# Causal attention with a gated feed-forward part on one core: transposes two steps behind the scores instead of three

## The reference, cut to what matters

```python
q = einsum('bse,hde->bhsd', x, Wq) + bq        # k and v in the same way
scores = einsum('bhsd,bhtd->bhst', q, k) / scale
scores = where(causal, -inf, scores)
att = softmax(scores, axis=-1) / scale
z = einsum('bhst,bhtd->bhsd', att, v)
return z.reshape(b, s, h * dh) @ proj
```

## Time and profile before

| what | value |
|---|---|
| median of three runs | 1347.55 us |
| the profiled execution's own time | 1347.42 us |
| its span, first to last instruction | 1345.7 us |
| PE busy | 1330.3 us, 99% of the span |
| DVE, ACT, POOL busy | 82%, 81%, 74% of the span |
| granted TensorE clock over the span | 1.000 of full speed |

### The profile page before, as it was taken

How to read it: one execution, slowest core, us unless ns; L and a number is a source line. 1 busy time by engine, 2 the same in 40 slices (tenths; PEclk the granted TensorE clock), 3 DMA queues, 4 the chain that set the end, 5 groups by cost and what they waited for, 6 DMA issues and landing times.

```text
span 1345.7 us, 34453 instructions
## 1 busy us (share of the span) xinstructions
PE 1330.3 (99%) x10783; PEld 1131.7 (84%) x10783; DVE 1106.3 (82%) x4001; ACT 1085.9 (81%) x3162; POOL 997.7 (74%) x1443
## 2 busy tenths in 40 slices
PE   7999999999999999999999999999999999999998
PEld 5788888888888888888888888888888888888887
DVE  8978888788787878878788787888878888788785
ACT  6887887888788887887888788788888887888785
POOL 7887777778777777777777768777677876778664
PEclk9999999999999999999999999999999999999999
DMA  6455444544544445454444544454454454545541
GB/s 155 95 119 118 103 112 113 122 104 111 125 107 116 105 113 123 103 122 110 116 103 115 123 103 115 112 122 110 103 124 113 103 122 112 122 95 119 118 103 48
DMA packets 112561, 150.59 MB, mean 112 GB/s; under 512 B 18239, under 2 KB 47230, under 8 KB 112382
## 3 DMA queue, kind: packets, MB, share of 16 engines
q1 hardware_dynamic: 111086, 147.97, 46.8%
q10 hardware_dynamic: 1296, 0.42, 0.2%
HBM read 10.69 MB, written 4.19 MB: 11 GB/s over the span
## 4 chain that ended last, share of the span: by engine, by line
PE 95%; ACT 1%; SPq 0%; POOL 0%; DVE 0%; DMA 0%; issue 0%; DVEq 0%; POOLq 0%
PE zp L1323 22%; PE ptp L1297 20%; PE jobp L1167 13%; PE scores L1285 9%; PE scores L1288 7%; PE outp L1335 7%; PE jobp L1172 6%; PE scores L1266 4%; PE scores L1263 3%; PE jobp L1182 1%; PE outp L1344 1%; PE jobp L1187 1%; PE jobp L1360 0%; PE jobp L1177 0%; ACT prob L721 0%; PE outp L1349 0%
## 5 line engine op out<-in xcount | busy, mean ns | idle before, releaser
L632 POOL TENSOR_TENSOR prob<-prob,rden 128x128 f32<-128x128 f32 (+3 forms) x1024 | 712.4, 720 | 247.2 <-DVE rden L971 240.7
L982 DVE CUSTOM_DVE_ANT_0 prob<-scores,mask 128x128 f32<-128x128 f32 (+3 forms) x1024 | 471.7, 488 | 199.8 <-issue 133.3
L721 ACT ACTIVATE prob<-prob,nmax 128x128 f32<-128x128 f32 (+3 forms) x1024 | 567.5, 559 | 12.1 <-DVE nmax L982 5.4
L1297 PE MATMUL ptp<-ident,prob 128*128 128x128 f32 x2560 | 366.9, 274 | 2.1 <-ACT pt L732 1.5
L1297 PEld LDWEIGHTS ptp<-ident,prob 128*128 128x128 f32 x2560 | 295.0, 140 | 27.4 <-POOL prob L632 5.0
L1323 PE MATMUL zp<-pt,v_sb 128*64 128x64 f32 (+3 forms) x4096 | 307.7, 303 | 0.0
L732 ACT ACTIVATE pt<-ptp 128x128 f32<-128x128 f32 (+3 forms) x512 | 221.2, 432 | 102.8 <-PE ptp L1297 102.8
L1323 PEld LDWEIGHTS zp<-pt,v_sb 128*64 128x64 f32 x4096 | 221.6, 137 | 51.2 <-issue 19.7
L994 DVE COPY pt<-ptp 128x128 f32<-128x128 f32 (+3 forms) x512 | 243.3, 475 | 3.9 <-PE ptp L1297 3.1
L571 POOL CAST k_low<-k_lo 64x512 fp32r<-64x512 f32 x256 | 156.0, 609 | 78.0 <-DVE k_lo L866 68.1
L1285 PE MATMUL scores<-k_twice,q_parts 128*128 128x384 f32 (+1 forms) x512 | 200.9, 392 | 0.0
(11 more groups left out here) (192 smaller groups left out, 2003.3 us busy)
## 6 DMA issues: line engine op xcount, KB each, us to landing
k_twice<-k_hi SPq DMA_DIRECT2D x506, 128.0 KB, 2.3
q_parts<-q_lo SPq DMA_DIRECT2D x256, 128.0 KB, 2.4
q_parts<-q_hi SPq DMA_DIRECT2D x254, 128.0 KB, 2.3
xin<-in_L_attn_x_dram SPq DMA_DIRECT2D x16, 256.0 KB, 3.1
xres<-in_L_attn_x_dram SPq DMA_DIRECT2D x16, 256.0 KB, 3.1
out_dram<-osb SPq DMA_DIRECT2D x15, 256.0 KB, 2.6
pt<-in_L_attn_Wq_dram SPq DMA_DIRECT2D x1, 512.0 KB, 4.8
pt<-in_L_attn_Wk_dram SPq DMA_DIRECT2D x1, 512.0 KB, 5.6
```

The lines of the kernel that those rows point to most:

```text
L632: nc.gpsimd.tensor_tensor(part, part, scale, ALU.mult).then_inc(pn_ready, 1)
L721: nc.scalar.activation(part, part, ACT.Exp, bias=nmax[:, s % NROT, h:h + 1], scale=-1.0, accum_out=den[:, s % NROT, h:h + 1]).then_inc(p_r ...
L982: nc.vector.tensor_tensor_reduce(out=prob[:, s % NROT, h, 0:cols], in0=scores[bank][:, first_col:first_col + cols], in1=mask[:, S - cols:S ...
L1297: done = nc.tensor.transpose(ptp[h][:, P * j:P * j + P], prob[:, s % NROT, h, P * j:P * j + P], ident[:])
```

## The change

LAG_T goes from 3 to 2. The transposes of unit s now stand in PE's step s+2, behind the scores of unit s+2, and the two copies of the transposed unit move with them on ACT and DVE. The value products keep their nine steps, and so do all other lags. The tail loses the transposes and copies of unit -3, since the last batch's own steps now reach that unit. The number of instructions on each engine stays the same.

```diff
-LAG_T = 3
+LAG_T = 2
...
-            evacuate_pt(c, -3)
             evacuate_z(c, -2)
             evacuate_pt(c, -2)
...
             reciprocals(c, -1)
-            evacuate_pt(c, -3)
             evacuate_pt(c, -2)
...
-            transpose(c, -3)
             project(c, -2, 2)
```

## The result

The changed kernel takes 1541.14 us (median of six runs, 1540.27 to 1543.08) against 1347.77 us for the kernel before (six runs, 1347.40 to 1348.26): a ratio of 1.1437, 95% interval 1.1423 to 1.1452. It is 193.4 us slower; forecast were 174.5 us more, 1522 in a range of 1465 to 1572. The profiled execution took 1542.95 us, with a span of 1541.2.

A forecast was written before the change was run, and what follows sets the result against it. PE, busy 1330.3 of 1345.7 us, was taken as the bound, so its waits are paid in full. Span 1345.7 + 159 (pairs) + 16 (once a batch) = 1520.7, plus 1.7 around it: 1522 us, range 1465 to 1572.

The forecast's parts named there:

- Which unit waits, where and for whom: PE's transposes of 512- and 256-column units wait for POOL's rows, 256 to 512 places, 150 to 200 us in total.
- Unit 15, 0.25 + 0.56: 512-column unit: PE's transposes wait 0.25 us for POOL's head 0 and 0.56 for head 1, together 0.81.
- Unit 17, 0.07 + 0.36: 256-column unit: PE's transposes wait 0.07 us for POOL's head 0 and 0.36 for head 1, together 0.43.
- Each pair pays again: DVE and POOL slip together with PE, so every pair of heads costs 1.24 us; 128 pairs cost 159 us.
- A single slip: Rival: after a first wait of about 1 us the engines stay ahead of PE; 1343 to 1348 us, chance 0.03.
- The ring: Rival: late transposes delay copies, exponentials, second maximum and next reciprocal; 50 to 90 us on top, 1575 to 1610, chance 0.12.
- Once a batch, +1.0 us: POOL's router products delay unit 3, +0.5 us; other steps an estimated +0.5; 16 us over 16 batches.
- Other widths nothing: Units of 128 and 384 columns: value products or 0.22 us more cover stand ahead of their transposes; counted as nothing.
- Second-order terms nothing: Wider DVE copies and ACT's copy ahead of the exponentials eat some 0.2 of 0.4 us slack; counted as nothing.
- The clock stays: PE keeps 2.4 GHz despite waits; the rival, a fall to 1.2 GHz throughout, meant above 2600 us, chance 0.02.
- The bounds: Lower: second heads alone, 0.95 a pair, 122 us, 1469; upper: 1.55 a pair, 1.6 more a batch, 224 us, 1572.
- the four rivals: Copies delaying reciprocals, 0.12; only second heads late, 1430 to 1450 us, 0.08; one slip only, 0.03; PE's clock falling, 0.02.

The follow-up runs named there:

- experiment 1: Changed kernel, with POOL multiplying only the first half of each head's columns: 1379.51 us.
- experiment 7: Changed kernel, with one more POOL multiplication of 128 columns, into an unread tile, ahead of each 512-column unit: 1582.63 us.
- experiment 2: Changed kernel, with DVE's reciprocals of 512- and 256-column units ahead of both maxima of the next unit: 1461.42 us.
- experiment 3: Changed kernel, with DVE's copy of the transposed head behind both maxima in steps with i = 3: 1540.94 us.
- experiment 4: Changed kernel, with PE's transposes of the 512-column unit between the value products of head 0 and head 1: 1556.03 us.
- experiment 10: Changed kernel, 512-column transposes behind both heads' value products, those units' copies last on DVE and ACT, 256-column reciprocal ahead of the next maxima: 1498.81 us.
- the best reordering: Changed kernel, 512-column transposes between the heads' value products, those units' copies last on DVE and ACT, 256-column reciprocal ahead of the next maxima: 1430.65 us.
- experiment 9: Kernel before (lag three), with value products cut in two around transposes and job, and that step's copies last on DVE and ACT: 1388.69 us.

## Why the prediction was right, step by step

- *Which unit waits, where and for whom.* Right. The waits are at the transposes, for POOL, in 514 places (256 to 512 forecast); their 219.1 us in the table are more than the 150 to 200 forecast. PE's busy time did not stay as it was either (93%, not 88%), since waits inside merged rows count as busy. The scores have small waits.
- *Unit 15, 0.25 + 0.56.* Measured 0.23 + 0.56. *Unit 17, 0.07 + 0.36.* Measured 0.06 + 0.35. All four were read from the kernel before, by laying POOL's end against PE's slot; experiments 1 and 7 show that the term is POOL's duration.
- *Each pair pays again.* Right: the waits recur in every pair, and the reciprocal keeps its place behind the scores. That POOL's start hangs on that place was argued from a bracket that names no engine ("issue"); experiment 2 shows it, where the earlier reciprocal takes the wait of most 256-column units away. A single slip would have shown one wait and no more.
- *The ring takes no part.* Right for the change: the reciprocal keeps 0.35 us of slack behind the exponentials in 512-column units (0.09 in unit 23), it waited for ACT only twice, and experiment 3 changed nothing. Experiments 4 and 10 show how near it is.
- *Once a batch, +1.0 us.* Right in size, mostly by luck: the waits of a batch (10.70) are 1.1 more than eight pairs at 0.79 + 0.41. Unit 3, forecast at 0.5 more, paid 1.07 where a typical unit pays 0.79, 0.28 more. Three things were not listed: unit 23 pays nothing, because in step 25, behind the extra products of step 24, PE comes late enough; unit 22, of 384 columns, pays 0.98 once a batch, since POOL starts it 0.82 later than usual after its reciprocal; units 9 and 25 pay 0.3 and 0.15 more ahead of head 0. "Other widths nothing" was wrong in that one unit.
- *Second-order terms nothing.* This is the step that failed, by about 20 us of 193. A typical step with i = 1 grew by 1.08 us: two more transposes 0.22, waits 0.79, and 0.07 that the sum did not have. Steps with i = 3 likewise. It comes to 0.72 a batch, 12 us. It goes with the waits: in experiment 1, which removes them, steps with i = 1 are 0.85 shorter, 0.79 and these 0.06. The other 8 us are scores behind step 26's transposes, which now wait for DVE's maxima, as these rows of PE and PEld of the changed kernel show:

```profile
851.67 0.38 PE L1295 MATMUL ptp<-ident,prob 128*128 128x128 f32 x2
852.24 0.50 PE L1283 MATMUL scores<-k_twice,q_parts 128*128 128x512 f32 x1 [0.19 <-DVE nmax L981]
...
852.24 0.19 PEld L1283 LDWEIGHTS scores<-k_twice,q_parts 128*128 128x128 f32 x1 [0.42 <-DVE nmax L981]
```

The scores of unit 27, 512 columns, go where those of unit 26 were, so they wait for unit 26's maxima. Step 26 has no job, and only the transposes stand between. Before, that was eight of unit 23; now it is two of unit 24, 0.66 us less cover. The step became 0.17 us shorter instead of 0.66. The prediction asked what each stall exposes, and did not ask what the transposes themselves had been covering where they left.

- *The clock stays.* Right in every batch but the first. Windows of the changed kernel there (length, busy PE, PEld, DVE, ACT, POOL, granted clock, DMA share, GB/s):

```profile
45.00:50.00 5.00, 4.19 (x25) 3.00 (x23) 4.11 (x16) 4.15 (x13) 4.92 (x7) 1.00 0.02 3
50.00:55.00 5.00, 3.92 (x34) 3.00 (x36) 3.03 (x11) 2.47 (x8) 2.42 (x5) 0.78 0.83 193
55.00:60.00 5.00, 4.87 (x26) 3.23 (x24) 2.09 (x9) 3.14 (x9) 2.73 (x5) 0.88 0.08 19
75.00:80.00 5.00, 4.54 (x21) 3.85 (x22) 1.96 (x7) 1.94 (x6) 4.95 (x6) 0.67 0.42 98
```

The granted clock lay at the 1.2 GHz level for part of three of these windows, the first time behind a stall of PE. In the timeline:

```profile
50.74 0.66 PE L1295 MATMUL ptp<-ident,prob 128*128 128x128 f32 x4 [1.22 <-POOL prob L632]
...
52.32 4.08 PE L1321 MATMUL zp<-pt,v_sb 128*64 128x64 f32 x32
```

32 value products took 4.08 us instead of 2.40. The rival had the mechanism, at some 4 us (below) instead of more than a thousand; over the span the clock was 0.998.

- *The bounds.* The lower one is not what its terms give: the second heads alone are 0.56 + 0.36 = 0.92 a pair at most, not 0.95, which makes 118 us and 1465 instead of 122 and 1469. Nor does the range hold "a bit of the neighbours": no rival's time lies between 1465 and 1572.
- *The path left out of the rivals.* None of the four rivals decided. Why the best reordering does not come back to the old time was in none of them either. Of its 83 us some 38 are the price of the cut, by experiment 9; by the lengths of its steps, unit 22's wait in step 24 and the waits in step 26 have 16 each.

## What to carry to other kernels

Before a consumer is moved nearer to its producer, read for each kind of unit where the consumer's slot will lie and when the producer ends, with its second piece laid against the consumer's first: once the first piece is late and the producer's piece takes longer than the consumer's, the second piece waits for the difference however late the first was, and it does so in every round if the producer's start hangs on the consumer. Ask also what the moved work covered where it stood. A wait pushed further down one engine's list is not gone; it moves to the engines whose lists stand behind its output, so move their places too, and price the seams that the cut makes.

## What the runs showed of the hardware

- **The clock does not follow from the longest wait alone.** In the kernel of experiment 3 PE has the same stall in the same place of the first batch, 1.22 us, and the granted clock there stays at 1.00. Its value products then take 2.40 us:

```profile
50.52 0.66 PE L1298 MATMUL ptp<-ident,prob 128*128 128x128 f32 x4 [1.22 <-POOL prob L632]
...
52.10 2.40 PE L1324 MATMUL zp<-pt,v_sb 128*64 128x64 f32 x32
```

  The two kernels' spans differ by 3.9 us (1541.2 and 1537.3), and their mean batches by 0.01. In experiment 10 the same wait of 1.54 us was followed by a fall in one batch and by none in the next, in one execution. The Trainium skill, page "TensorE: Matmul & The Clock Gate", section "Part 1: The HAM clock gate (the 'warmup' mystery)", makes activity what releases the throttle; the fall behind a stall agrees with that, and why the clock fell in one place and not in the other stays open.
- **Changing between 64-column value products and 128-column transposes has a price:** 0.30 us for one more pair of changes a step (experiment 9), with no wait shown. What in PE takes it, no run shows.
- **A stalled PE loses a little more than it waits:** about 0.06 us in each step with a wait, gone with the waits in experiment 1. That the weights can only be loaded after the wait is my reading of it; no run tested that.
